# Delta-rule layers on one core: a loop turn of four heads in place of eight, and the step matrix squared ahead

## The reference, cut to what matters

```python
def delta_rule(q, k, v, beta):
    def step(W, inp):
        qt, kt, vt, bt = inp
        wk = jnp.einsum('bhde,bhe->bhd', W, kt)
        v_new = bt * (vt - wk)
        W = W + jnp.einsum('bhd,bhe->bhde', v_new, kt)
        out = jnp.einsum('bhde,bhe->bhd', W, qt)
        return (W, out)
    W0 = jnp.zeros((bsz, H, D, D), dtype=q.dtype)
    _, outs = jax.lax.scan(step, W0, (q, k, v, beta))
    return outs

def fast_ff(x, ln_g, ln_b, slow_w, out_w):
    h = layer_norm(x, ln_g, ln_b)
    qkvb = jnp.einsum('sbi,oi->sbo', h, slow_w).reshape(slen, bsz, H, 3 * D + 1)
    q, k, v, beta = jnp.split(qkvb, [D, 2 * D, 3 * D], axis=-1)
    q = jax.nn.softmax(q, axis=-1); k = jax.nn.softmax(k, axis=-1)
    beta = jax.nn.sigmoid(beta)
    attn = delta_rule(q, k, v, beta)
    o = jnp.einsum('sbd,od->sbo', attn.reshape(slen, bsz, H * D), out_w)
    return x + o
```

## Time and profile before

| what | value |
|---|---|
| time, median of 3 runs | 5363.59 us (5357.72 to 5369.23) |
| profiled execution, its own time | 5342.08 us |
| its span | 5340.3 us |
| granted PE clock, mean of the span | 0.84 of full |
| first delta-rule stage, from its weight DMA to that of the next stage | 328.73 to 1103.65 us |
| second one | 1478.0 to 2474.49 us |

### The profile page before, as it was taken

How to read it: one execution, slowest core, us unless ns; L and a number is a source line. 1 busy time by engine, 2 the same in 40 slices (tenths; PEclk the granted TensorE clock), 3 DMA queues, 4 the chain that set the end, 5 groups by cost and what they waited for, 6 DMA issues and landing times. The chain is left out here.

```text
span 5340.3 us, 166254 instructions
## 1 busy us (share of the span) xinstructions
PE 4097.5 (77%) x71052; PEld 2447.9 (46%) x71053; DVE 2742.2 (51%) x5139; ACT 1867.5 (35%) x3387; POOL 874.9 (16%) x2195
## 2 busy tenths in 40 slices
PE   3677667679965555556788887699999999985995
PEld 1235555534344444444345555245455454443663
DVE  3444444330233322333578887388686886864343
ACT  1121111112211111111366665167575775741221
POOL 0000000000000000000255554011111111102112
PEclk7787777779966666667899998799999999996997
DMA  1000000000000000000100000000000000005223
GB/s 42 2 8 3 3 3 3 4 19 0 0 10 5 5 5 5 5 5 5 38 1 1 1 1 1 10 1 0 1 0 1 1 0 1 0 3 194 86 85 101
DMA packets 47646, 87.35 MB, mean 16 GB/s; under 512 B 7120, under 2 KB 38128, under 8 KB 46064
## 3 DMA queue, kind: packets, MB, share of 16 engines
q1 hardware_dynamic: 40944, 61.84, 3.4%
q0 software_dynamic: 6144, 16.79, 1.0%
HBM read 45.05 MB, written 33.55 MB: 15 GB/s over the span
## 5 line engine op out<-in xcount | busy, mean ns | idle before, releaser
L1656 PE MATMUL psum<-hm_ex,hm_mix 128*128 128x512 f32 x1024 | 510.1, 621 | 42.5 <-ACT hm_Aq L1736 38.5
L1722 ACT ACTIVATE hm_ex<-psum,hm_nm 128x1024 f32<-128x1024 f32 x256 | 285.6, 1116 | 296.2 <-DVE hm_nm L1780 296.1
L658 PE MATMUL psum<-fw_M,fw_qkTc 32*32 32x32 f32 x8192 | 134.4, 236 | 283.4 <-issue 283.4
L1790 DVE TENSOR_SCALAR_CACHE_REDUCE hm_plus<-hm_Aq,hm_cbcol,hm_sums 128x1024 f32<-128x1024 f32 x256 | 340.6, 1330 | 0.0
L1795 DVE COPY hm_A<-psum 128x1024 f32<-128x1024 f32 x256 | 312.9, 1222 | 51.4 <-PE psum L1665 48.1
L1656 PEld LDWEIGHTS psum<-hm_ex,hm_mix 128*128 128x128 f32 x1024 | 175.5, 191 | 351.2 <-issue 343.4
L1780 DVE TENSOR_REDUCE hm_nm<-psum 128x1 f32<-128x1024 f32 x256 | 311.1, 1215 | 11.5 <-PE psum L1644 11.5
L1665 PEld LDWEIGHTS psum<-K,hm_Aq 128*128 128x128 f32 x2048 | 236.7, 140 | 149.9 <-issue 145.3
L665 PE MATMUL psum<-fw_w,fw_stage 128*128 128x512 f32 (+1 forms) x512 | 290.7, 707 | 16.0 <-DMA fw_w<-in_slow 16.0
L1727 ACT ACTIVATE hm_junk<-hm_Aq 128x1024 f32<-128x1024 f32 x256 | 270.6, 1057 | 30.3
L1644 PE MATMUL psum<-hm_kt,hm_qd 64*32 64x512 f32 x4096 | 278.3, 602 | 0.0
(11 more groups left out here) (365 smaller groups left out, 8116.0 us busy)
## 6 DMA issues: line engine op xcount, KB each, us to landing
ex_rows_in<-ex_zero SPq DMA_DIRECT2D x2, 5120.0 KB, 24.6
ex_xs<-ex_rows_in SPq DMA_DIRECT2D x80, 128.0 KB, 2.0
ex_rows_out<-ex_ys SPq DMA_DIRECT2D x80, 128.0 KB, 1.7
ex_w<-in_ex_w SPq DMA_DIRECT2D x2, 4096.0 KB, 21.2
X<-in_x SPq DMA_DIRECT2D x2, 2048.0 KB, 12.3
out_y<-X SPq DMA_DIRECT2D x2, 2048.0 KB, 9.0
ff_w<-in_ff_w SPq DMA_DIRECT2D x2, 1024.0 KB, 5.7
pt_w_proc<-in_pt_proc SPq DMA_DIRECT2D x1, 2048.0 KB, 7.7
```

What stands on the lines that cost most here:

```text
L658: mm = pe.matmul(to(n)[rows(b), :], by(n)[rows(b), :], of(n)[rows(b), :], start=start and (stop or n == 0), stop=stop)
L1656: mm = pe.matmul(bank[4 + c], mix[:, u, :], ex[:, u, 512 * c:512 * c + 512], start=True, stop=True)
L1722: act.activation(ex[:, u, :], flat2(psum[:, 2 * u:2 * u + 2, :]), ACT.Exp, bias=nm[:, u:u + 1], accum_out=rsum[:, u:u + 1]).then_inc(s_ex, 1)
L1790: dve.tensor_scalar(plus[:, :], Aq[:, u, :], cbcol[:, :], sums[:, :], ALU.add, ALU.add, accum_out=sums[:, :]).then_inc(s_run, 1)
```

## The change

A turn of the loop (a "unit") now works four of the eight heads of a tile, and a tile takes two units, so a layer has 64 units (NU). Each half of the heads has its own state `M[:, a]`, and the halves take turns. The instructions of a unit have half the columns of those of a turn before, or half their count on PE.

On PE the loop over units is a loop of two turns (`pe.Fori(0, 2) as a`) within a loop over tiles, so the code of one unit serves both halves. The other engines hold two bodies in their loop. The projection of a unit is one group of 388 columns in bank 0, with weights laid out by half.

The recurrence now needs two step products after z3: y0 = r0 + nt r0, and U = y0 + nt^2 y0. The square n2 is made ahead: DVE transposes nt (`turned`), PE multiplies (`s_n2t`), ACT copies (`s_n2`). So per unit there are again 13 `tiles` steps on PE. The three masked products of the lower matrix become one DVE operation of three parts (`lows`). ACT gets two more copies, n2 and Mc (a copy of the state, which `th` and `rd` now read). One masked constant ("off") and the order of the slow weights on the host change.

```diff
-        QKN = 2 * C
+        G, CG = HEADS // 2, C // 2
+        QKN, WN = 2 * CG, 3 * CG + HEADS // 2
+        NU = 2 * NT
...
                     if rc:
-                        pe.wait_ge(s_m, r + 1)
                         pe.wait_ge(s_ct, r + 1)
+                        pe.wait_ge(s_mc, r + 1)
                         pe.sem_inc(s_go, 1)
-                        chain(lambda n: qkTc[:, HEADS + n, :], M, s_th)
-                        tiles(lambda n: bank[6][:, cols(n)], lambda n: qkTc[:, n, :], of(M), s_rd, stop=False)
+                        tiles(to(4), lambda n: qkTc[:, G + n, :], of(Mc), s_th)
+                        tiles(to(6), lambda n: qkTc[:, n, :], of(Mc), s_rd, stop=False)
+                        pe.wait_ge(s_nn, r + 1)
+                        pe.sem_inc(s_go, 1)
+                        tiles(to(1), of(nn), of(nt), s_n2t)
...
-                        chain(of(z3), u0, s_so)
+                        tiles(to(4), of(z3), of(u0), s_so)
                     if nxt:
-                        pe.wait_ge(s_staged, i + 2)
-                        project(i + 1, 0, QKN, 0, s_pq)
+                        pe.wait_ge(s_staged, t + 2 if isinstance(a, int) and a == 1 else t + a + 1)
+                        project(a)
...
-                        pe.wait_ge(s_rk, r * 2 + 1)
+                        pe.wait_ge(s_n2, r + 1)
+                        pe.wait_ge(s_y0, r + 1)
                         pe.sem_inc(s_go, 1)
-                        chain(of(nt), rk, s_so)
-                    if nxt:
-                        project(i + 1, QKN, 3 * C + HEADS, 1, s_pv)
+                        tiles(to(4), of(n2), of(y0), s_so)
...
-                bodies(body, pe)
+                for i in range(-1, 2):
+                    body(i, i // 2, i % 2, True, i >= 0, i >= 1)
+                with pe.Fori(1, NT - 1) as j:
+                    with pe.Fori(0, 2) as a:
+                        body(j * 2 + a, j, a, True, True, True)
+                for i in range(NU - 2, NU + 1):
+                    body(i, i // 2, i % 2, i + 1 < NU, i < NU, True)
...
 (ACT)
+                        act.wait_ge(s_n2t, r + 1)
+                        act.activation(flat(n2[:, :, :]), bank[1][:, 0:CG], ACT.Copy).then_inc(s_n2, 1)
...
+                        act.wait_ge(s_m, i if since(i, 1) else 1)
+                        act.activation(flat(Mc[:, :, :]), flat(M[:, a, :, :]), ACT.Copy).then_inc(s_mc, 1)
...
 (DVE)
-                    own.mark(dve.tensor_tensor(l8[:, :, :], pairs[:, :, 1, :], small(1), ALU.mult))
-                    own.done(dve.tensor_tensor(l8t[:, :, :], pairs[:, :, 1, :], small(0), ALU.mult))
-                    dve.tensor_tensor(zl[:, 0, :, :], small(2), l8t[:, :, :], ALU.subtract).then_inc(s_l8, 1)
-                    dve.tensor_tensor(loff[:, :, :], pairs[:, :, 1, :], off, ALU.mult).then_inc(s_lo, 1)
+                    dve.tensor_tensor(lows[:, :, :, :], pairs[:, :, 1, :].unsqueeze(1).broadcast_to([P, 3, G, STEP]),
+                                      parts, ALU.mult).then_inc(s_l8, 1)
+                    dve.wait_ge(s_l8, i + 1)
+                    dve.tensor_tensor(zl[:, 0, :, :], small(2), l8t, ALU.subtract).then_inc(s_z1, 1)
...
+                def turned(i):
+                    dve.wait_ge(s_nt, i + 1)
+                    dve.transpose(flat(nn[:, :, :]), flat(nt[:, :, :])).then_inc(s_nn, 1)
```

More of the change, by code:

```diff
@@ L593, in fast_weight_stage @@
         dif = sb("dif", [P, QKN]); ex = sb("ex", [P, QKN])
-        eb = sb("eb", [P, 3, HEADS]); power = sb("power", [P, 2, HEADS])
-        qk = sb("qk", [P, QKN]); qkT = sb("qkT", [P, 2 * HEADS, STEP]); vh = sb("vh", [P, C])
-        kc = sb("kc", [P, C]); qkTc = sb("qkTc", [P, 2 * HEADS, STEP]); vhc = sb("vhc", [P, C])
-        compact = lambda n: sb(n, [P, HEADS, STEP])
-        l8, l8t, loff, l2, l4, z2, z3, nt, qm = (compact(n) for n in "l8 l8t loff l2 l4 z2 z3 nt qm".split())
-        zl = sb("zl", [P, 2, HEADS, STEP])
@@ new lines, in fast_weight_stage @@
+        qk = sb("qk", [P, QKN]); qkT = sb("qkT", [P, 2 * G, STEP]); vh = sb("vh", [P, CG])
+        kc = sb("kc", [P, CG]); qkTc = sb("qkTc", [P, 2 * G, STEP]); vhc = sb("vhc", [P, CG])
+        compact = lambda n: sb(n, [P, G, STEP])
+        l2, l4, z2, z3, nt, nn, n2, qm = (compact(n) for n in "l2 l4 z2 z3 nt nn n2 qm".split())
+        lows = sb("lows", [P, 3, G, STEP])
+        l8t, l8, loff = (lows[:, y, :, :] for y in range(3))
+        u0, r0, y0, U, Mc, att = (compact(n) for n in "u0 r0 y0 U Mc att".split())
@@ L611, in fast_weight_stage, with units @@
         tokens = lambda i: H[:, :, :].rearrange("p h (b s) -> p h b s", b=B)[:, :, :, bass.ds(i * STEP, STEP)]
-        def bodies(body, eng, start=None):
+        def units(body, eng, start=None):
             for i in range(-1, 2):
-                body(i, i + 1 < NT, i >= 0, i >= 1)
-            with eng.Fori(2, NT - 1) as i:
+                body(i, i // 2, i % 2, True, i >= 0, i >= 1)
+            with eng.Fori(1, NT - 1) as j:
                 if start:
                     start()
-                body(i, True, True, True)
+                for a in range(2):
+                    body(j * 2 + a, j, a, True, True, True)
             if start:
                 start()
-            for i in range(NT - 1, NT + 1):
-                body(i, i + 1 < NT, i < NT, True)
+            for i in range(NU - 2, NU + 1):
+                body(i, i // 2, i % 2, i + 1 < NU, i < NU, True)
         def since(i, n):
@@ L650, in _ @@
                 pool.wait_ge(s_power, 2)
-                bodies(body, pool, own.clear)
+                units(body, pool, own.clear)
             @block.tensor
@@ L677, in fourth @@
                 def fourth():
-                    for n in range(HEADS):
+                    for n in range(G):
                         for b in range(B):
@@ L755, in body @@
                             pe.wait_ge(s_fin, r)
[L756 to L759 removed]
+                        pe.transpose(bank[7][:, 0:P], flat(att[:, :, :]), k.const("ident")).then_inc(s_ot, 1)
                 pe.wait_ge(s_w, 16)
[L762 removed]
+                for i in range(-1, 2):
+                    body(i, i // 2, i % 2, True, i >= 0, i >= 1)
@@ L909, in body @@
                         softmax(i + 1)
-                dve.memset(M[:, :, :], 0.0).then_inc(s_m, 1)
+                    if ch:
+                        turned(i)
+                dve.memset(M[:, :, :, :], 0.0).then_inc(s_m, 1)
                 dve.wait_ge(s_m, 1)
-                bodies(body, dve, own.clear)
+                units(body, dve, own.clear)
 @stage
@@ L2350, in layout @@
         cols = [w[:, DH * q:DH * q + DH].reshape(C, C) for q in range(3)] + [w[:, 3 * DH]]
-        out[f"slow{n}"] = rows(np.concatenate(cols, 0).T)
+        part = lambda g: np.concatenate([c.reshape(2, -1, C)[g] for c in cols], 0)
+        out[f"slow{n}"] = rows(np.concatenate([part(1), part(0)], 0).T).reshape(P, CH, 2, -1)
         out[f"fo{n}"] = rows(a["L2_attn_fw_out_w"][n].T)
```

196 lines of the change are left out of this document (97 added, 99 removed).

## The result

The changed kernel took 9268.4 us (median of 4 runs, 9264.1 to 9328.05) against 5363.4 us for the kernel before in the same measurement: ratio 1.7306, 95% interval 1.7234 to 1.7379. The forecast was 4778 us. The two delta-rule stages did become shorter, by 463 us together. Elsewhere 4386 us came in, in a stretch that the change doesn't touch.

What follows compares the result with a forecast made beforehand. PE's code supply was taken to bound the delta-rule stages; each would take 20 + 60 + 505 + 8 = 593 us, saving 585, so 4757 plus 21.5 for the median of runs gives 4778 us, range 4690 to 5045.

Steps and rivals of the forecast that it cites:

- The remaining 3569 us of the span stay.: Everything outside the two delta-rule stages was taken to keep its time, 3569 us of the 5340.3 us span.
- Supply of code: Delta-rule stages: PE's instruction fetch bounds them; a 54 KB loop is kept, 108 KB fetched; packets fall from 430 to under 100.
- Price of a unit: Delta-rule loop with code at hand: closed PE-DVE loop sums to 8.44 us, taken as 8.7, bounds 8.4 and 9.3.
- the rival: Delta-rule loop: PE's clock is not held, projection costs 2.9 for 1.4, about 10.9 us a unit, 5033 us; chance 0.14.
- The forecast, at 0.72: Main case: code kept, granted clock 0.9 or more in the delta-rule loop, 4778 us, own range 4700 to 4900; chance 0.72.
- the lead of 20 us and the tail of 8 us: Each delta-rule stage: time before the first u0 28.6 us now, taken as 20; behind the last u0 15, halved to 8.
- Both stages last equally long: Sign to look for: the two delta-rule stages take the same time, 593 us each by the sum.
- u0's spacing of 8.4 to 9.6 us: Sign in the delta-rule loop: DVE's u0 comes every 8.4 to 9.6 us; over 10 us the prediction is wrong.
- The code is not kept: Rival: each delta-rule unit pays branch and code fetch, at least 15.4 us, 998 us a stage, 5590 us; chance 0.07.
- The outer branch misses: Rival: PE's inner loop stays, but code is refetched once in two units, 420 us more, 5200 us; chance 0.04.
- the third product comes back as the square: Delta-rule unit: the dropped step product (0.60 + 0.42 and hand-overs a tile) returns as the square; the shortened path doesn't close the loop.

Runs made afterwards that it cites:

- The hinted loop: Kernel before with only the toolchain's hint about the branch back (`hint_back_edge=True`) on PE's loop of the delta stages: 4592.1 us.
- place 0: Kernel before with only PE's delta-stage loop moved, its first instruction at the first place of a 256-instruction fetch block: 4596.6 us.
- the version without the block: Changed kernel with the flag's load and the conditional exact search behind the pattern stage taken out: 4879.6 us, ratio to before 0.9078.
- The filled run: Changed kernel without the conditional exact search, five unused matmuls on constants per unit filling PE's waits: 4797.3 us, ratio to before 0.8909.
- the written-out version: Changed kernel without the conditional exact search, PE's inner loop over the halves unrolled, 108 KB of code a turn: 5266.95 us.
- the search by pairs: Kernel before, PE's loop at the start of a fetch block, doubt kept per pair of tiles so one doubtful pair is searched alone: 4599.9 us, ratio 0.8568.
- place 220: Kernel before with only PE's delta-stage loop moved, its head at slot 220 of a 256-instruction fetch block: 5552.2 us.

## Why the prediction was wrong, and where it was right

**The step that failed** is "The remaining 3569 us of the span stay." I had read which instructions are issued outside the two stages, in a trace in which the block was skipped, and took that they don't depend on the change. The source has one branch on data there, and what it reads comes from the stages whose arithmetic the change reorders: the squared step matrix, and sums of halves. None of the rivals had it, so the range could not hold the time. Had I read the source from the changed stages to the end for branches, the price could have been had only roughly: a path that didn't run has no row. The chance would have stayed a guess as well. The runs now give one tie in six sets of roundings, and a price of 4389 us. A case of that kind belongs among the rivals even at 0.1.

**Supply of code: right in its effect, incomplete in its reason.** Packets in the two stages fell from 430 to 33 in the changed kernel, by the queue's lines in the two stages:

```profile
q8 instruction: 16, 0.26, 0.2%
...
q8 instruction: 17, 0.28, 0.2%
```

I argued by size, 54 KB kept and 108 KB not. The runs show that 108 KB are kept too: in seven blocks without a hint (509 us, 26 packets), and in eight with one (509 us, 26 packets). In eight blocks without a hint they are fetched in every turn or in every second one. The bound that I named was right, and halving the loop is one way around it, but not the cheapest. The hinted loop of eight blocks has a DMA share of 0.00 from 500 to 600 us. That loop and the one at place 0 branch back over some 1,700 instructions, six blocks and more, and between 400 and 800 us, 24,111 and 24,104 matmuls or some 29 turns' worth, only 3 and 4 packets come. Why the unhinted loops of eight blocks fetch in each turn, or in every second, is not shown.

**Price of a unit: nearly right at full clock.** The timeline of the changed kernel for one unit in the second stage, some of its rows, start and length:

```profile
1700.16 0.29 DVE L885 TENSOR_TENSOR fw_u<-fw_vhc,psum 128x128 f32<-128x128 f32 x1 [0.38 <-PE psum L665]
...
1701.52 1.56 PE L671 MATMUL psum<-fw_w,fw_stage 128*128 x4
...
1703.54 0.29 DVE L891 TENSOR_TENSOR fw_y<-psum,fw_r 128x128 f32<-128x128 f32 x1 [1.32 <-PE psum L665]
...
1704.94 0.65 PE L687 MATMUL psum<-fw_zl,fw_l 32*32 32x64 f32 x32 [0.56 <-issue]
...
1705.55 1.01 POOL L652 TENSOR_TENSOR fw_eb<-fw_eb,fw_power 128x4 f32<-128x4 f32 x1
...
1707.45 0.45 PE L665 MATMUL psum<-fw_z,fw_lows 32*32 32x32 f32 x32 [0.47 <-DVE fw_z L876]
...
1708.63 0.27 DVE L880 STREAM_TRANSPOSE fw_nn<-fw_nt 128x128 f32<-128x128 f32 x1
1708.84 0.29 DVE L885 TENSOR_TENSOR fw_u<-fw_vhc,psum 128x128 f32<-128x128 f32 x1
```

From u0 to u0 it is 8.68 us; I had taken 8.7. But that is the quicker half of a pair: the next u0 starts at 1718.04, 9.20 us on. The terms are near: a step of 32 columns (L665) 0.45 where 0.30 + 0.14 stood, `fourth` (L687) 0.65 where 0.57 stood, four projecting matmuls 1.56 where 1.4 stood, u0 0.29, the transpose 0.27 for 0.32. DVE's longest waits in that stage are in front of y0 (99.8 us) and of the lower matrix (L854, 73.1 us), then of `fourth`'s transpose (41.1 us); I had named y0 and `fourth`. POOL's power took 1.01 us for 4 columns, between my bounds of 0.2 and 1.64, and nobody waits for it. The slower half of each pair is a term that I put at nothing: with both halves written out and the code kept, most units take 8.6 to 8.8 us, so my estimate is that the 0.4 us or so belong to the outer loop, of which there is one turn for two units. What the split costs also shows: two units 17.7 us against 13.8 us for the turn of eight heads. The changed structure is slower work per tile, and it gained only because before's stall was larger.

**The clock: in part the rival.** The forecast, at 0.72, stood on a granted clock of 0.9 or more in the loop. The tile view of u0 in the two stages:

```profile
L885 DVE TENSOR_TENSOR fw_u<-fw_vhc,psum x64: 249/286/289, 350.8 to 1003.9; 128x128 f32<-128x128 f32 x64
...
L885 DVE TENSOR_TENSOR fw_u<-fw_vhc,psum x64: 247/286/290, 1408.7 to 2003.0; 128x128 f32<-128x128 f32 x64
```

The means are (1003.9 - 350.8)/63 = 10.4 us and (2003.0 - 1408.7)/63 = 9.4 us. In windows of the changed kernel, 100 us of each stage, then parts of one unit of the first:

```profile
630.00:730.00 100.00, 81.92 (x4082) 64.19 (x4082) 54.24 (x194) 30.27 (x115) 12.60 (x23) 0.83 0.00 0
1688.00:1788.00 100.00, 79.41 (x4636) 63.06 (x4631) 61.69 (x221) 34.64 (x132) 15.24 (x29) 0.97 0.00 0
...
596.00:601.00 5.00, 3.33 (x250) 2.84 (x245) 4.19 (x17) 2.29 (x9) 1.55 (x3) 1.00 0.00 0
601.00:602.00 1.00, 1.00 (x84) 0.96 (x76) 0.39 (x2) 0.08 (x1) 0.00 (x0) 0.71 0.00 0
602.00:603.00 1.00, 1.00 (x60) 1.00 (x51) 0.23 (x1) 0.20 (x1) 0.00 (x0) 0.50 0.00 0
605.00:606.00 1.00, 1.00 (x66) 0.57 (x64) 0.04 (x1) 0.00 (x0) 0.00 (x0) 1.00 0.00 0
```

In the first stage the clock falls to 0.50 within 601 to 602, while PE works without a pause on the square; in the 5 us before, PE was busy for 3.33. It stays low through gram and z3 on u0 and most of the projection, which takes 2.42 us in place of 1.56, and is at 1.00 again from 605 to 606. So it goes in unit after unit: 0.83 in the mean and 10.5 and 9.9 us in turn. My rival, at 0.14, had the low clock's price in the whole unit, 10.9 us. What happened lies between it and the forecast, in one stage, and mostly not in the other. The pattern can set in within a stage: in the version without the block the second stage takes 9.2 us a unit for 18 units after its first two, and then 10.2 to its last ones.

**The terms that were mis-sized.** Saved were 463 us where 585 stood, 122 us less. The filled run, whose clock is 1.00 in the loop, puts a size on each part. Its stages of 612 us are 19 us each above the 593 forecast, 38 in all: the first two and last two units take 55 us where 48 stood, the 59 between them 525 us (8.9 each) where 517 stood, and the lead of 20 us and the tail of 8 us are 22 and 11. The changed kernel's stages lie 684.6 - 612.2 = 72 and 624.0 - 611.3 = 13 us above the filled ones: 85 us for the clock. 38 + 85 = 123. Without the block the kernel measured 4880 us, inside my range of 4690 to 5045, and 102 us above the point. So the reading of the two stages held to within the range; its point was too low by the clock and by the terms above.

**The other signs and rivals.** "Both stages last equally long" failed (684.6 and 624.0 us), as did u0's spacing of 8.4 to 9.6 us in the first stage (10.4). "The code is not kept" gave 5590 us and 998 us a stage; it did not come in the changed kernel, and what it describes is what the written-out version shows in its second stage, at 1088 us. "The outer branch misses" did not come: 33 packets in all. That the third product comes back as the square and gives nothing was nearly right: 0.16 us a unit without the filling.

**What stays open:** how often roundings make a tie; why a stage falls into the pattern with the low clock or out of it; why a loop of eight blocks is fetched in every turn at three places and in every second turn at one; and what the hint changes so that it isn't fetched at all.

## What to carry to other kernels

Before pricing a change of arithmetic, search the source behind it for branches on data: the path that didn't run has no row in the profile, and a tie within one pair of tiles cost 4390 us here, so keep the exact fallback as narrow as the doubt (340 us for a pair of tiles). When PE waits for "issue" and its code queue moves packets all through a loop, try the hint on its branch back, or count the blocks that the loop touches and move its head, before restructuring the work: the moved head gave 14.3% (with the search by pairs, 3 us slower than the place alone) and the hint as much in its one run, where halving the loop gave 9.2%. And compare a new structure with the old one freed of its stall, not with the stalled one.

## What the runs showed of the hardware that was not expected

- The place of a loop in the code's blocks (16.4 KB a packet) is worth a factor of 1.94 in a stage: 509.0 us with the head at place 0, 989.8 us at place 220, for the same 26,944 matmuls.
- One instruction a turn, the hint on the branch back, does as much without moving the loop: 509.1 and 508.7 us a stage, 26 packets each, in a loop that touches eight blocks by the stalls of its first pass.
- A loop of 108 KB on PE runs turn after turn without fetching (DMA share 0.00; at place 0, 4 of the stage's 26 packets come between 400 and 800 us), and then holds the clock at 1.00 with 13.8 us a turn, below the quick turn of before (14.68 us at 0.84).
- A loop of 9 to 10 us with PE busy for some 80 us in 100 shows either of two patterns for tens of units, with the clock at 0.83 or at 0.97. Five matmuls of filling in a unit hold it at 1.00: 4880 to 4797 us.
- `MAX8` and `MATCH_REPLACE8` on 128x1024 take 1228 and 1208 ns (960 of each; the page's means of 1127 and 1107 mix in those on 128x512). 37 of each a tile make 2.6 ms of the 4.4 that the exact search takes.
